# Per-sample weights and a residual on one core: 2 KB weight runs, one bias table, row loads issued by ScalarE, and products of zeros between the plan's products

## What is computed

```
def reference(x, cat, W, b):        # x (128,64,256), cat (128,), W (64,256,256), b (64,256)
    return x + einsum('bsd,bdh->bsh', x, W[cat]) + b[cat][:, None, :]
```

## Time and profile before

| | us |
|---|---|
| median of three runs | 99.18 |
| lowest and highest of them | 98.57, 100.05 |
| the profiled execution's own time | 99.0 |
| its span in the trace | 97.0 |

### The profile page before, as it was taken

How to read it: one execution, slowest core, us unless ns; L and a number is a source line. 1 busy time by engine, 2 the same in 40 slices (tenths; PEclk the granted TensorE clock), 3 DMA queues, 4 the chain that set the end, 5 groups by cost and what they waited for, 6 DMA issues and landing times.

```text
span 97.0 us, 3027 instructions
## 1 busy us (share of the span) xinstructions
PE 85.5 (88%) x788; PEld 58.1 (60%) x788; DVE 53.6 (55%) x130; ACT 55.1 (57%) x98; POOL 34.3 (35%) x65
## 2 busy tenths in 40 slices
PE   0318969999998699999999999999999999999980
PEld 0107735676666466666767575868666866676640
DVE  2792407648236275748575475655187519664840
ACT  1402284692537282985866760977278827885500
POOL 5400000000000028999969623939702493000000
PEclk9999999999999999999999999999999999999999
DMA  0899999999999999998999999999996679999563
GB/s 13 261 345 365 348 349 346 350 346 349 350 347 349 348 350 325 341 356 267 402 367 402 365 400 370 388 388 367 329 355 252 220 171 392 409 372 343 170 209 108
DMA packets 19970, 31.25 MB, mean 322 GB/s; under 512 B 1521, under 2 KB 15986, under 8 KB 19954
## 3 DMA queue, kind: packets, MB, share of 16 engines
q0 software_dynamic: 4640, 16.26, 46.6%
q1 hardware_dynamic: 13602, 13.18, 42.3%
q10 hardware_dynamic: 1712, 1.64, 5.2%
HBM read 25.30 MB, written 8.39 MB: 347 GB/s over the span
## 4 chain that ended last, share of the span: by engine, by line
PE 62%; ACT 1%; DVE 0%; issue 0%; ACTq 0%; SPq 0%
PE mm_ps L598 42%; PE xt_ps L507 11%; PE mm_ps L584 6%; PE xt_ps L598 2%; ACT w_slot L337 1%; DVE rows L477 0%; PE xt_ps L584 0%; ACTq L337 0%; SPq L208 0%
## 5 line engine op out<-in xcount | busy, mean ns | idle before, releaser
L598 PE MATMUL mm_ps<-w_slot,xT 128*64 128x256 f32 x496 | 57.1, 380 | 2.1 <-ACT w_slot L337 2.1
L337 ACT COPY w_slot<-w_all 128x512 f32 x64 | 38.4, 619 | 28.6 <-POOLq L208 9.2
L598 PEld LDWEIGHTS mm_ps<-w_slot,xT 128*64 128x64 f32 x496 | 34.5, 137 | 19.1 <-issue 2.1
L477 DVE TENSOR_TENSOR rows<-mm_ps,rows 128x512 f32<-128x512 f32 (+1 forms) x32 | 21.6, 674 | 24.9 <-PE mm_ps L598 24.5
L337 DVE COPY w_slot<-w_all 128x512 f32 x64 | 27.2, 453 | 7.5 <-SPq L208 4.1
L192 POOL DMA_DIRECT2D w_all<-in_L_cond_W x32 | 16.4, 514 | 39.5 <-DMA w_all<-in_L_cond_W 32.2
L507 PE MATMUL xt_ps<-ident,rows 128*128 128x128 f32 x128 | 18.5, 293 | 2.3 <-DMA rows<-in_x 2.3
L349 ACT COPY xT<-xt_ps 128x512 f32<-128x512 f32 x32 | 17.2, 584 | 5.5 <-PE xt_ps L507 5.5
L507 PEld LDWEIGHTS xt_ps<-ident,rows 128*128 128x128 f32 x128 | 15.0, 150 | 7.3 <-issue 4.8
L584 PE MATMUL mm_ps<-bias_parts,is_sample 96*64 96x256 bf16 x124 | 9.9, 278 | 0.0
L223 POOL DMA_DIRECT2D out<-rows x11 | 8.7, 790 | 1.1 <-SPq L208 0.6
(11 more groups left out here) (53 smaller groups left out, 12.5 us busy)
## 6 DMA issues: line engine op xcount, KB each, us to landing
w_all<-in_L_cond_W POOLq DMA_DIRECT2D x32, 256.0 KB
w_all<-in_L_cond_W SPq DMA_DIRECT2D x29, 256.0 KB, 5.6
out<-rows POOLq DMA_DIRECT2D x11, 512.0 KB, 7.1
rows<-in_x POOLq DMA_DIRECT2D x9, 512.0 KB, 6.6
rows<-in_x SPq DMA_DIRECT2D x6, 512.0 KB, 6.6
out<-rows SPq DMA_DIRECT2D x8, 256.0 KB, 5.1
w_all<-in_L_cond_W ACTq DMA_DIRECT2D x3, 256.0 KB, 5.5
rows<-in_x ACTq DMA_DIRECT2D x1, 512.0 KB, 4.3
```

The costliest lines, as they stand in the source:

```text
L337: copy(w_slot[:, PAIR * p + half, :, :].rearrange("p k h -> p (k h)"), w_all[:, bass.ds(c, 1), :, :].rearrange("p c k h -> p (c k h)")).th ...
L477: V.tensor_tensor(to, sums, to, ALU.add).then_inc(sums_added, 1)
L598: last = T.matmul(to[HALF * half:HALF * (half + 1), :], xT[:, slot, k, j, :], w_slot[:, j, k, :], start=False, stop=(k == K - 1), skip_gro ...
```

## The change

- Weight matrices are loaded as one run of 2 KB to a partition: partition p holds rows 2p and 2p + 1. To match, the transposes take every second column of the rows (`k::K`) in place of 128 adjacent ones.
- Rows 0 and 1 are issued by ScalarE first of all; rows 2 by SP; rows 3, 4, 5 and 6 by ScalarE, behind its copies of groups 0, 1, 2 and 3. SP issues no rows in its loop. ScalarE's loads are 0, 4 and 7 in place of 0, 6 and 7.
- One bias table: the bias is loaded once, split in three on 64 partitions, and one mask `has_category` serves 12 products (3 to a tile, each 32 rows high) before group 0. `slot_words` is read on VectorE behind the first split. POOL clears no masks.
- ScalarE reads the slots before the halves of group 0, and those of group 1 only behind the copies of group 0's third pair; a half of group 1 is copied behind each of its first two pairs.
- 21 products of zeros (128 x 128, bfloat16) run on TensorE: 8 before the plan's first products, 6, 2 and 5 in its next three gaps.

```
-ACT_LOADS = (0, 6, 7)
+ACT_LOADS = (0, 4, 7)
+KEEP_BUSY = (8, 6, 2, 5)
-PLAN_STEPS = {"samples": 6, "cats": 7, "first": 10, "list": 13, "slots": 16, "bias": 21}
+PLAN_STEPS = {"samples": 6, "cats": 7, "first": 10, "list": 13, "slots": 16, "bias": 18}
-X_AFTER_LOAD = {3: 13, 4: 19, 5: 25, 6: 31, 7: 33, 8: 37, ...}
+X_AFTER_LOAD = {7: 33, 8: 37, ...}
+X_AFTER_COPIES = {0: 3, 1: 4, 2: 5, 3: 6}
...
-                             weights[bass.ds(c, 1), :, :].rearrange("c (k p) h -> p (c k) h", p=P), **how
+                             weights[bass.ds(c, 1), :, :].rearrange("c (p k) h -> p (c k) h", k=K), **how
...
-            sp.dma_start(bias_nat[0:C, :], bias).then_inc(bias_loaded, 16)
-            load_rows(sp, 0)
+            sp.dma_start(bias_nat[:, :], bias).then_inc(bias_loaded, 16)
             load_rows(sp, 2)
...
                 load_weights(sp, n, part(word, n % WORD))
-                rows_after(sp, n)
...
-            pool.memset(in_two[:, :, :, :], 0.0).then_inc(masks_set, 1)
-            pool.memset(in_third[:, :, :, :], 0.0).then_inc(masks_set, 1)
...
-            act.dma_start(bias_nat[C:PAIR * C, :], bias).then_inc(bias_loaded, 16)
+            load_rows(act, 0)
             load_rows(act, 1)
...
+            act.wait_ge(plan_read, 2)
+            slots = slots_of(mybir.EngineType.Activation, 0, 1)
             for k in range(K):
                 x_half(0, k)
             for n in ACT_LOADS[1:]:
                 load_weights(act, n, part(word, n % WORD))
-
-            act.wait_ge(plan_read, 2)
-            slots = slots_of(mybir.EngineType.Activation, 0, 1)
...
-                if g + 1 < GROUPS:
+                if 0 < g < GROUPS - 1:
                     slots = slots_of(mybir.EngineType.Activation, g + 1, 1)
                 for p in range(PAIRS_IN_GROUP):
                     copy_weights(act, nc.scalar.copy, now[p], g, p, 1, odd_weights_ready)
-                    if g == 0 and p == 1:
-
-                        for k in range(K):
-                            x_half(1, k)
+                    if g == 0 and p < K:
+
+                        x_half(1, p)
+                    elif g == 0 and p == K:
+                        slots = slots_of(mybir.EngineType.Activation, 1, 1)
+                if g in X_AFTER_COPIES:
+                    load_rows(act, X_AFTER_COPIES[g])
...
+            split(V.tensor_copy(bias_first[:, :], bias_nat[:, :]))
+
             dve.wait_ge(plan_products, 4)
             V.tensor_copy(slot_words[:, :], slot_words_ps).then_inc(plan_read, 1)
+            split(V.tensor_tensor(bias_rest[:, :], bias_nat[:, :], bias_first[:, :], ALU.subtract))
+            split(V.tensor_copy(bias_second[:, :], bias_rest[:, :]))
+            V.tensor_tensor(bias_third[:, :], bias_rest[:, :], bias_second[:, :], ALU.subtract).then_inc(plan_step, 1)
+            V.tensor_scalar(has_category[:, :], mm_ps[3][0:C, 0, 0:B], iota_part[0:C, 0:1], None, ALU.is_equal
+                            ).then_inc(plan_step, 1)
...
-                    last = T.transpose(xt_ps[g % XT_SLOTS][k][:, p, :], rows[:, g % X_SLOTS, p, k * P:(k + 1) * P],
+                    last = T.transpose(xt_ps[g % XT_SLOTS][k][:, p, :], rows[:, g % X_SLOTS, p, k::K],
                                        ident[:, :])
...
+                for n, bias_part in enumerate((bias_first, bias_second, bias_third)):
+                    last = T.matmul(bias_ps[t][TILE * n:TILE * (n + 1), :], has_category[:, TILE * t:TILE * (t + 1)],
+                                    bias_part[:, :], start=True, stop=True, skip_group_check=True)
+                return last
+
+            def keep_busy(n):
+
+                for _ in range(n):
+                    T.matmul(xt_ps[1][0][:, 0, :], idle[:, :], idle[:, :], start=True, stop=True,
+                             skip_group_check=True)
...
-            bias_of_tile(0).then_inc(plan_products, 1)
+            for t in range(TILES):
+                last = bias_of_tile(t)
+            last.then_inc(plan_products, 1)
```

More of the change, by code:

```diff
@@ L32 @@
 FAR = 1000.0
-PLAN_STEPS = {"samples": 6, "cats": 7, "first": 10, "list": 13, "slots": 16, "bias": 21}
-X_AFTER_LOAD = {3: 13, 4: 19, 5: 25, 6: 31, 7: 33, 8: 37, 9: 40, 10: 43, 11: 46, 12: 47, 13: 51, 14: 53, 15: 60}
+PLAN_STEPS = {"samples": 6, "cats": 7, "first": 10, "list": 13, "slots": 16, "bias": 18}
+X_AFTER_LOAD = {7: 33, 8: 37, 9: 40, 10: 43, 11: 46, 12: 47, 13: 51, 14: 53, 15: 60}
+X_AFTER_COPIES = {0: 3, 1: 4, 2: 5, 3: 6}
 STORE_AFTER_LOAD = {0: 37, 1: 40, 2: 43, 3: 46, 4: 48, 5: 51, 6: 59}
@@ L94, in build_cond_residual @@
         ahead_or_self = sb("ahead_or_self", [P, P], BF16)
+        idle = sb("idle", [P, P], BF16)
         iota_part = sb("iota_part", [P, 1])
@@ L112, in build_cond_residual @@
         place_powers = sb("place_powers", [P, WORD], BF16)
-        in_two = sb("in_two", [PAIR * C, TILES, SPLITS, TILE], BF16)
-        in_third = sb("in_third", [C, TILES, SPLITS, TILE], BF16)
+        has_category = sb("has_category", [C, B], BF16)
         load_words = sb("load_words", [1, LIST_WORDS + 1], I32)
         slot_words = sb("slot_words", [1, SLOT_WORDS], I32)
-        bias_nat = sb("bias_nat", [PAIR * C, H])
-        bias_rest = sb("bias_rest", [PAIR * C, H])
-        bias_two = sb("bias_two", [PAIR * C, H], BF16)
+        bias_nat = sb("bias_nat", [C, H])
+        bias_rest = sb("bias_rest", [C, H])
+        bias_first = sb("bias_first", [C, H], BF16)
         bias_second = sb("bias_second", [C, H], BF16)
@@ L143, in build_cond_residual @@
         cat_col_ps = mm_ps[3][:, 0, B:B + 1]
-        bias_ps = [mm_ps[2 + t // PAIR][0:ROWS, t % PAIR, :] for t in range(TILES)]
+        bias_ps = [mm_ps[2 + t // PAIR][:, t % PAIR, :] for t in range(TILES)]
         cats_loaded = sem("cats_loaded")
@@ L149, in build_cond_residual @@
         consts_ready = sem("consts_ready")
+        idle_set = sem("idle_set")
         ones_set = sem("ones_set")
@@ L398, in _ @@
             V = nc.vector
+            V.memset(idle[:, :], 0.0).then_inc(idle_set, 1)
             V.memset(ones_f[:, :], 1.0).then_inc(ones_set, 1)
@@ L438, in _ @@
             assert steps[0] == PLAN_STEPS["slots"]
-            dve.wait_ge(bias_loaded, 32)
+            dve.wait_ge(bias_loaded, 16)
             splits = [0]
@@ L446, in split @@
                 dve.wait_ge(bias_step, splits[0])
[L448 to L464, removed]
+            split(V.tensor_copy(bias_first[:, :], bias_nat[:, :]))
             dve.wait_ge(plan_products, 4)
             V.tensor_copy(slot_words[:, :], slot_words_ps).then_inc(plan_read, 1)
+            split(V.tensor_tensor(bias_rest[:, :], bias_nat[:, :], bias_first[:, :], ALU.subtract))
[3 more added lines that the diff above has]
+                            ).then_inc(plan_step, 1)
+            steps[0] += 2
+            assert steps[0] == PLAN_STEPS["bias"]
             dve.wait_ge(plan_read, 2)
@@ L470, in put_tile @@
             def put_tile(t):
-                V.tensor_copy(bias_parts[:, t, :], bias_ps[t]).then_inc(bias_ready, 1)
+                V.tensor_copy(bias_parts[:, t, :], bias_ps[t][0:ROWS, :]).then_inc(bias_ready, 1)
             dve.wait_ge(plan_products, 5)
@@ L481, in _ @@
                 if p >= 1:
-                    dve.wait_ge(tiles_made, 1 if p == 1 else TILES - 1)
                     put_tile(p)
@@ L511, in bias_of_tile @@
             def bias_of_tile(t):
[L513 to L516, removed]
+                for n, bias_part in enumerate((bias_first, bias_second, bias_third)):
[6 more added lines that the diff above has]
+                             skip_group_check=True)
+            pe.wait_ge(idle_set, 1)
+            keep_busy(KEEP_BUSY[0])
             pe.wait_ge(plan_step, PLAN_STEPS["cats"])
@@ L521, in _ @@
             T.matmul(cat_col_ps, cats[:, :], ones_row[:, 0:1], start=True, stop=True).then_inc(plan_products, 1)
+            keep_busy(KEEP_BUSY[1])
             pe.wait_ge(plan_step, PLAN_STEPS["first"])
@@ L524, in _ @@
             T.matmul(place_ps, ahead_or_self[:, :], is_first[:, :], start=True, stop=True).then_inc(plan_products, 1)
+            keep_busy(KEEP_BUSY[2])
             pe.wait_ge(plan_step, PLAN_STEPS["list"])
@@ L530, in _ @@
             T.matmul(loads_ps, is_first[:, :], ones[:, :], start=True, stop=True).then_inc(plan_products, 1)
+            keep_busy(KEEP_BUSY[3])
             pe.wait_ge(plan_step, PLAN_STEPS["slots"])
@@ L601, in group @@
                     last.then_inc(pairs_done, 1)
-                    if g == 0 and pair == 0:
-                        for n in range(1, TILES):
-                            bias_of_tile(n).then_inc(tiles_made, 1)
             for g in range(GROUPS):
```

2 lines of the change are left out of this document (removed).

## The result

The changed kernel takes 100.23 us (median of 4 runs, 99.42 to 100.9), the kernel before beside it 98.88 (98.39 to 100.05): a ratio of 1.0138, 95% interval 1.0092 to 1.0184. It is 1.4% slower; 96.8 was forecast. The profiled execution took 100.22 with a span of 98.3, 1.3 us more than before.

A forecast was written before the change was run, and what follows sets the result against it. Loads were taken to bound the kernel up to group 5, PE behind it. At load 31, -2.2 (2 KB runs) - 0.5 (start and reports) + 0.5 (rows) gave -2.2 us: 99.0 - 2.2 = 96.8 us, range 95.0 to 99.2.

The forecast's parts named there:

- What bounds: Whole kernel: loads bind before 34.16 us, and from there PE runs without a pause at 5.03 us a group.
- 2 KB runs: Weight loads: about 383 GB/s in place of 348, saving 1.75 us up to load 25 and 2.2 for 32 loads.
- rival 2: Rows 5, 6 and likewise 12 come late for PE; rows 5 and 6 cost about 1.1 us: 97.9 us; chance 0.12.
- The strided transposes: Transposes in all groups: taken as costing nothing; bounds nothing to half speed, 0.95 us a group, 14 us in all.
- Rival 3: Transposes' strided weight load is slower: decides from 18 ns each, 111 us at half speed; chance 0.08.
- Rows on the other queue: Rows 5 and 6 on ScalarE's queue take turns with weights, delaying load 25 by 0.8 us and load 31 by 0.5.
- What I cost at nothing: Before and in group 0: PE's early work, 21 zeros and twelve bias products, taken as hidden by slack, adding nothing.
- The early work of PE: Group 0 would end near 16 in place of 18.37 us, with 2.4 us given back by group 3's waits.
- The start: First loads: rows of group 0 first on ScalarE's queue and one bias copy less, together 0.5 us (0.2 to 0.8).
- SP's reports: Group 3, loads 24 and 25: without rows in SP's loop their reports come 0.5 us sooner (0 to 0.6).

The follow-up runs named there:

- start and bias: Changed kernel with 1 KB runs, adjacent columns, rows 3 to 6 on SP's queue and no zeros, against the kernel before: 99.01 us, ratio 1.0022.
- the rate alone: Kernel before with 2 KB runs and transposes of adjacent columns left as they were: 97.81 us, ratio 0.9884 to the kernel before.

## Why the prediction was wrong

The parts, each by its ratio to the kernel before:

| what is in | ratio | 95% interval |
|---|---|---|
| rate of 2 KB runs | 0.9884 | 0.9804 to 0.9964 |
| stride | 1.0169 | 1.008 to 1.0257 |
| both of these | 0.9989 | 0.9957 to 1.0022 |
| start and bias | 1.0022 | 0.9985 to 1.0058 |
| zeros | 1.0001 | 0.9963 to 1.0038 |
| all but rows 3 to 6 on ScalarE | 1.0012 | 0.9977 to 1.0048 |
| all but the stride | 0.9963 | 0.992 to 1.0006 |
| all but both of these | 0.9863 | 0.9795 to 0.993 |
| all | 1.0138 | 1.0092 to 1.0184 |

So the stride gives back what the rate brings, start, bias and zeros bring nothing that shows, and the place of rows 3 to 6 makes the kernel slower than before. The measured 100.23 lies 3.4 us above the forecast 96.8. Without the stride and with the rows on SP's queue the kernel takes 97.64. So 2.6 us of the miss are these two together, both put too low in the sum (the stride alone 1.5 to 1.7 us, the place of the rows 1.25), and the 0.8 us left over are early gain that was put too high.

- **What bounds.** Right for the kernel before: loads up to group 5, PE alone behind it. Not carried through to the faster loads: with 2 KB runs and stride alone PE has no wait behind group 0, so an early gain is also capped by PE's own path, and the stride counts there too.
- **2 KB runs.** Forecast 383 GB/s, measured 379 and 376 with the runs alone, so the rate was right to 2%. The model under it, a fixed cost of each packet, is less sure: the measured rates give it as 7 to 8 ns and not 8.5, and 3.5 KB packets for rows 3 to 6 did not raise the rate. The Trainium skill's 358 GB/s for the HBM side ("DMA: Bandwidth & Descriptors", "Where 436 GB/s comes from"), which it gives as half of what one HBM stack has for its two cores, did not bind here: those windows are reads alone, of a kernel on one core. But the forecast's 2.2 us at group 5 became 0.94 us at the end. Where it went is seen in one trace only: group 5 began 2.05 us earlier, and rows 14 took 1.15 of them back. The prediction had named such a wait for rows 12, in rival 2, and left it out of the sum.
- **The strided transposes: the step that failed first.** The sum took nothing, "as no resource in these rows is full at 128 ns a transpose". That was the error: the weight loads of the transposes had 140 ns each in the records of the kernel before, longer than the 128 ns from one transpose to the next, so they were the thing with least room. Measured: 208 ns a load, 0.13 us a group, 1.21 us from group 5 on in the traces, and 1.46 us by the medians with the stride alone. Rival 3 had the mechanism and a chance of 0.08. Its point of decision, 2.2 us / 120 = 18 ns a transpose, was set wrong: only 80 of the transposes stand behind the start of group 5, so there it would take 28 ns to use up 2.2 us. At the measured 16 ns the stride would have left some of the forecast 2.2 us; it took all of the 0.94 us that came. The bounds, nothing and half speed, were right, and between ends so far apart the value should not have been the end. The Trainium skill's note ("SBUF — State Buffer", cachelines of 16 bytes: two hits on a line are enough) would have it free; for this operand the measured load differs from it, and the measurement decides.
- **Rows on the other queue: the second step that failed.** The sum took 0.8 us for what they push back at load 25, and gave their own lateness a chance of 0.12. Measured: 1.25 us for the placement, and 1.0 in each of two other pairs of kernels (2 KB runs and adjacent columns, 0.9963 and 0.9863; 1 KB runs, 1.0123 and 1.0022, where the zeros differ too). Load 25 was in fact reported near 31.6 (ScalarE's copy at 31.68), close to the forecast 31.3; it was rows 5 that stood last. Rival 2 sized their lateness at 0.5 where it was 1.37. It counted on an issue near 25.5, and the issue came at 26.99: it hangs on load 19, and the rows that had gone before on ScalarE's queue had pushed that back from 25.69 to 26.81. Its reason, the smaller share of a 1 KB packet, is not needed: with 1 KB packets on both queues rows 5 were late as well.
- **What I cost at nothing.** The early work of PE was cover and not gain, as said. The start, which the sum did count with 0.5 us, brought load 25 in 0.59 us sooner and nothing that the ratio shows at the end. The zeros hid in their gaps: with them alone in the kernel, SP's first load left when it had before. That TensorE would be at full speed for the first transposes, near 5.6 us, was wrong: they took 1.98. It cost group 0 some 2 us; what it cost the end no run shows by itself.
- **SP's reports.** The prediction gave 0.5 us to them, and no run changes them by themselves, but the traces show them. Before, load 25 landed at 32.51 and was copied at 33.40, 0.89 us later; in the changed kernel it landed at 31.54 and was copied at 31.68. So 0.75 us were won there. With rows on SP's queue the delay mostly stands: 0.89 us in the kernel with the rest of the change, 1.19 with the rate alone, 1.24 with start and bias alone, but 0.19 with runs and stride alone. So SP's own order is a rival to the DMA as what bounds group 3, and an order in which SP reports before it issues rows 6 was not tried.

## What to carry to other kernels

A layout that makes a transfer cheaper is paid for by whoever reads it: here 1.2% was won in a stage that ends at group 5 and 1.7% paid over all the groups (both to within 0.9), and the two together came out level. Price the reader's step over the whole kernel before the writer's gain in one stage. Moving a part of the transfers to a second queue gave full DMA engines no bandwidth here: rows 4 and 5 landed after 9.42 and 8.32 us where they had taken 6.49 and 6.63, and in three pairs of kernels the weights on SP's queue took longer to land with rows on ScalarE's (6.4 us against 5.4, 6.6 against 5.5, 5.6 against 5.2). So what is needed last must be issued earlier by that much, and an issue that hangs on a load is late when the load is. And look for the next chain of transfers before counting a gain at the front: in one trace it took 1.15 of 2.05 us back, in another, with 1.16 us, nothing.

## What was not expected of the hardware

- A weight load of 128 x 128 floats with a step of two floats: 208 ns against 140. In a row of eight transposes 1.15 us against 1.02.
- 2 KB packets moved pure reads at 376 to 379 GB/s from 10 to 30 us (rate alone) where 1 KB packets stood at 348 and 349. Rows 3 to 6 in packets of 3.5 KB beside 1 KB weights: 341 to 356.
- Rows issued by ScalarE beside SP's stream took 9.4 us (rows 4) and 8.3 (rows 5) to land, where the same transfers behind SP's own loads took 6.5 and 6.6 before.
- 21 products of zeros over 4 us did not make the first eight transposes fast: 1.97 to 1.98 us with them and without. The moment at which TensorE got fast was anywhere from about 8 to 17 us, with a granted clock that read 1.00 all along in most profiles. In one it was fast at 8.68 us and at a granted 0.56 and 0.50 from 11 us on, with idle gaps of 0.50 us before 8.68 and 1.66 before 11.99.
